# The state product of a linear-attention sequence: one 128-column matmul, or four 32-column tiles of the array

## What is computed

```python
xn = _layernorm(x, axis=-1)
x = x + attn(xn, ...) + ffn(xn, ...)
```

```python
o_int = jnp.einsum('bhtd,bhde->bhte', qc * jnp.exp(gcc)[..., None], S)
kd = kc * jnp.exp(gtc[..., None] - gcc)[..., None]
S = jnp.exp(gtc)[..., None, None] * S + jnp.einsum('bhtd,bhte->bhde', kd, vc)
```

## Time and profile before

| | |
|---|---|
| median of 3 runs | 410.85 us (409.74 to 411.74) |
| profiled execution, its own time | 410.52 us |
| span of its instructions | 408.6 us |
| granted TensorE clock, mean | 0.991 |
| PE busy | 386.7 us (95%) |
| DVE, ACT, POOL busy | 326.3, 304.5, 276.6 us |
| matmuls of the state, L747 | 64 records of 377 ns (median) |
| DVE's copy of the state, L1468 | 32 of 425 ns (median) |

### The profile page before, as it was taken

How to read it: one execution, slowest core, us unless ns; L and a number is a source line. 1 busy time by engine, 2 the same in 40 slices (tenths; PEclk the granted TensorE clock), 3 DMA queues, 4 the chain that set the end, 5 groups by cost and what they waited for, 6 DMA issues and landing times.

```text
span 408.6 us, 13495 instructions
## 1 busy us (share of the span) xinstructions
PE 386.7 (95%) x3650; PEld 337.1 (83%) x3651; DVE 326.3 (80%) x868; ACT 304.5 (75%) x947; POOL 276.6 (68%) x237
## 2 busy tenths in 40 slices
PE   7988899999999999999999999899999999999990
PEld 6656788877788888888888878799999999999990
DVE  5989898999988898889888888667687687687750
ACT  4889998787887978797888887466666676666660
POOL 6012534268888888888888833178888888888884
PEclk9999999999999999999999999999999999999996
DMA  8846586464555445474655340145545555455530
GB/s 237 230 158 193 177 288 245 120 186 129 170 179 162 128 127 168 143 200 140 186 155 154 115 137 14 44 63 69 69 68 65 66 69 67 63 67 71 64 32 0
DMA packets 59096, 51.29 MB, mean 126 GB/s; under 512 B 7200, under 2 KB 51392, under 8 KB 59072
## 3 DMA queue, kind: packets, MB, share of 16 engines
q1 hardware_dynamic: 45936, 42.07, 36.0%
q0 software_dynamic: 12272, 8.54, 15.1%
q10 hardware_dynamic: 864, 0.40, 0.4%
HBM read 33.14 MB, written 18.30 MB: 126 GB/s over the span
## 4 chain that ended last, share of the span: by engine, by line
PE 80%; DVE 6%; ACT 4%; DMA 3%; issue 3%; POOL 2%; SPq 1%; ACTq 0%; DVEq 0%; POOLq 0%
PE psA L912 16%; PE psVG L900 16%; PE psVG L721 9%; PE psO L756 8%; PE psA L737 7%; PE psT L790 6%; PE psQK L709 6%; PE psT L782 4%; PE psKS L747 3%; PE psO L770 3%; ACT E L1080 2%; SPq L343 1%; DMA x_all<-in_L_attn_x_dram 1%; DMA gcB<-decay_rows 1%; PE psQK L891 1%
## 5 line engine op out<-in xcount | busy, mean ns | idle before, releaser
L579 POOL DMA_INDIRECT out_dram<-yw,sidx x71 | 115.0, 1619 | 29.1 <-issue 11.6
L538 POOL TENSOR_TENSOR rms<-msn,neg_half 128x8 f32<-128x8 f32 x32 | 53.3, 1665 | 48.4 <-DVE msn L1412 44.7
L1080 ACT ACTIVATE E<-gcB,ngc 128x128 f32<-128x128 f32 x256 | 78.5, 397 | 0.4 <-DMA gcB<-decay_rows 0.4
L544 POOL DMA_INDIRECT sorted_rows<-x_all,pos_i x64 | 65.2, 1019 | 14.4 <-issue 10.5
L531 POOL TENSOR_SCALAR_AFFINE_SELECT E<-E 128x1024 f32<-128x1024 f32 x32 | 35.7, 1115 | 33.5 <-ACT E L1080 33.2
L756 PEld LDWEIGHTS psO<-v_sb,pr 128*64 128x64 f32 x1024 | 39.8, 137 | 12.0 <-issue 4.1
L756 PE MATMUL psO<-v_sb,pr 128*64 128x64 f32 x1024 | 44.5, 225 | 2.7 <-DVE pr L1440 2.5
L1089 ACT ACTIVATE sq<-psO 128x512 f32<-128x512 f32 x32 | 19.1, 597 | 33.4 <-PE psO L756 33.4
L1440 DVE TENSOR_TENSOR pr<-psA,E 128x512 f32<-128x512 f32 x64 | 41.0, 682 | 0.2
L912 PE MATMUL psA<-xT_all,v_sb 128*128 x288 | 38.3, 276 | 0.5 <-issue 0.4
L900 PE MATMUL psVG<-xgT,gcB 128*128 128x128 f32 x288 | 38.6, 277 | 0.0
(11 more groups left out here) (197 smaller groups left out, 928.5 us busy)
## 6 DMA issues: line engine op xcount, KB each, us to landing
gcB<-decay_rows SPq DMA_DIRECT2D x32, 512.0 KB
sorted_rows<-blank SPq DMA_DIRECT2D x12, 396.0 KB, 5.5
xg<-sorted_rows SPq DMA_DIRECT2D x71, 66.0 KB
x_all<-in_L_attn_x_dram SPq DMA_DIRECT2D x16, 256.0 KB, 5.3
out_dram<-res SPq DMA_DIRECT2D x32, 128.0 KB
eqB<-decay_exp_rows SPq DMA_DIRECT2D x32, 64.0 KB
w1b<-in_L_ffn_w_dram SPq DMA_DIRECT2D x8, 256.0 KB
xT_all<-in_L_ffn_w_dram SPq DMA_DIRECT2D x32, 64.0 KB
```

The source lines that it names most:

```text
L538: nc.gpsimd.tensor_tensor(rms[:], msn[:], neg_half[:, 0:2 * H], ALU.pow).then_inc(rms_ready, 1)
L544: nc.gpsimd.indirect_dma_start(out=sorted_dram, out_offset=bass.IndirectOffsetOnAxis(ap=pos_i[:, t:t + 1], axis=0), in_=x_all[:, t, :], in ...
L579: nc.gpsimd.indirect_dma_start(out=out_rows, out_offset=bass.IndirectOffsetOnAxis(ap=sidx[j][:], axis=0), in_=yw[j][:], in_offset=None, bo ...
L1080: last = nc.scalar.activation(E[j][:, k, h * P:(h + 1) * P], gcB[j][:, k * H + h, :], ACT.Exp, bias=ngcf[:, bass.ds((s * 2 + k) * H + h, 1)])
```

## The change

The one matmul of `state` becomes four, one for each head. Head h has as stationary operand its own 32 columns of `kd` and as moving operand its own 64 columns of `v_sb`; the output goes to partitions 32h to 32h+31 of the bank, so each is a tile of 128 rows and 32 columns of the array. All four write the same 64 columns (256 to 319). Only the last one raises `s_ready`. The three other products of a head's keys with another head's values are not computed any more.

DVE's `copy_state` stays one instruction with the same number of output elements (128x256). It reads the 64 columns four times (a broadcast over the four blocks of `S_sb`) and multiplies with the same mask.

```diff
                 pe.wait_ge(kd_ready, s + 1)
                 pe.wait_ge(v_copied, s + 1)
-                nc.tensor.matmul(psKS[:, HV:2 * HV], kd[:], v_sb[j][:, 0, :], start=True, stop=True).then_inc(s_ready, 1)
+                for h in range(H):
+                    last = nc.tensor.matmul(psKS[h * DK:(h + 1) * DK, HV:HV + DV], kd[:, h * DK:(h + 1) * DK], v_sb[j][:, 0, h * DV:(h + 1) * DV],
+                                            start=True, stop=True)
+                last.then_inc(s_ready, 1)
...
                 dve.wait_ge(s_ready, s + 1)
                 if not (isinstance(i, int) and s == 0):
                     dve.wait_ge(o_ready, s)
-                nc.vector.tensor_tensor(S_sb[:], psKS[:, HV:2 * HV], headmask[:], ALU.mult).then_inc(s_copied, 1)
+                nc.vector.tensor_tensor(S_sb[:].rearrange("p (h d) -> p h d", d=DV), bc(psKS[:, HV:HV + DV].unsqueeze(1), [P, H, DV]),
+                                        headmask[:].rearrange("p (h d) -> p h d", d=DV), ALU.mult).then_inc(s_copied, 1)
```

## The result

The changed kernel took 417.44 us (median of 4 runs, 416.9 to 419.17). The kernel before took 411.3 us beside it (4 runs, 409.74 to 412.12). The ratio is 1.0165, with a 95% interval of 1.0133 to 1.0198: slower by 6 us. The forecast was 410.9, with a range to 413.2, so it was wrong. The same two kernels were later run beside each other three times more. Twice the change cost about the same again (1.0155 and 1.0132), and once it cost nothing (0.998). Why it does both is what the experiments are about; they show where the 6 us go, and leave open what sets it off.

What follows compares the result with a forecast made beforehand. PE was taken as the bound, busy all 90.00 us of the attention window. The profiled 410.52 us, +0.5 for PE and -0.3 for DVE, gave 410.7; with the median 0.33 higher, 410.9, range 408.8 to 413.2.

Steps and rivals of the forecast that it cites:

- The price of the tiles: PE's queue around the state: net +0.01 us per state, between -0.04 and +0.08, taken as +0.5 us in all.
- All three terms: Per state on PE: border into the tiles +0.09 us, state itself -0.18, exposed weight load of the next product +0.10.
- Rival 2: State on PE: no borders or exposed loads, so packing saves 0.32 us each; 401.2 us, chance 0.03.
- Rival 4: State on PE: short tiles run one behind the other, +0.30 us per state; 420 us, chance 0.03.
- What `S_sb` gives: DVE's copy of the state starts 0.18 us earlier, which helps from 77.35 to 93 us: -0.3 us in all.
- In the loop this buys nothing, as PE doesn't wait for DVE there: DVE's copy in the loop: its start, 0.18 us earlier, gains no time.
- ends at 143.61, ahead of its reader on PE: DVE's `res`, in the same chain as the state's copy, is done before the PE line L782 needs it.
- rival 1: Second half of L756: the earlier state clears PE's stalls in some 24 steps, -2.9 us; 408.0 us, chance 0.08.
- Rival 3: Borders around the state cost more, +0.08 us each, 413.3 us; or PE's stalls grow, 413.8; chance 0.15.

Runs made afterwards that it cites:

- `a_again`: The changed kernel, unaltered, run again beside the kernel before at another time: 409.29 us, ratio 0.998.
- `b_again`: The kernel before, unaltered, run again for its trace: 408.82 us, ratio 1.0002.
- `a_third`: The changed kernel, unaltered, run a third time beside the kernel before: 417.39 us, ratio 1.0155.
- `a_fourth`: The changed kernel, unaltered, run a fourth time on one more chip as the yardstick: 417.63 us, ratio 1.0132.
- `e14_shift_before`: The kernel before with the output projection's signal raised by a later matmul, 0.27 us later, same work: 417.09 us, ratio 1.0113.
- `e5_diag`: The changed kernel with its four tiles written in the diagonal blocks and DVE reading 256 columns as in the kernel before: 409.32 us, ratio 1.0012.
- `e3_maskfirst_after`: The changed kernel with POOL's mask moved ahead of the three indirect stores of a step: 431.91 us, ratio 1.0486.
- `e8`: State as one matmul for sequences 0 to 11, four diagonal-block tiles from 12 on, DVE as in the kernel before: 408.74 us, ratio 1.0007.
- `e9`: State as four diagonal-block tiles for sequences 0 to 11, one matmul from 12 on, DVE as in the kernel before: 408.88 us, ratio 1.0003.
- `e12_two_tiles`: The kernel before with projection ahead of the state, two 64-column state tiles, outputs' own halves together, `on` ahead of `S_sb`: 413.14 and 414.57 us.

## Why the prediction was wrong, point by point

**The price of the tiles: right.** All three terms came to within 5 ns (table above): +90, -181 and +105 ns make +14, where +10 was forecast. The step is 6 or 7 ns shorter all the same, since the row from L709 to L721 takes some 24 ns less in `a_again` than in `b_again`; nobody forecast that, and no run says why. That the step comes out so near to no change is in part luck. Rival 2, for which the Trainium skill spoke ("TensorE: Matmul & The Clock Gate", "Measured speedup vs the span model"), is refuted. The rule holds inside the group as far as the stream goes, with the four tiles starting 6 or 7 ns apart here and not 4; it has no term for the changes of shape on either side, 0.09 and 0.09 + 0.10 us, and these eat the gain. Rival 4 is refuted too: eight records take 0.25 with the border.

**What `S_sb` gives: right but small.** It starts 0.15 us earlier against the last L721 (0.705 behind it and not 0.859), where 0.18 was forecast; the 0.3 us can't be seen in the scatter of the start-up stretch.

**The step that failed** is the sentence "In the loop this buys nothing, as PE doesn't wait for DVE there", with the one on `res`, which "ends at 143.61, ahead of its reader on PE". Both are true of the earlier trace rows. But they rest on a signal that arrives as its matmul ends. `res` has some 0.7 us to spare before it delays the transposes, and with the holds of 0.90 to 1.25 us it starts 1.15 to 1.40 us behind the projection and not 0.29, so 0.9 to 1.1 later. I looked at how much work was ahead of each wait and not at how much delay each wait could stand, and who could cause one.

**The second fault** is in rival 1. The profile of before had a hint: stalls of 0.1 to 0.25 us with no work to explain them. I put them down to DVE's and POOL's work lying over L756, and allowed as much change as they had size (2.9 us in either direction). `b_again` shows that they vanish altogether where no signals are held: 6.893 in place of 7.005 us. With the signals of L756 late by 0.07 to 0.47 us in the same profile, I take them for the mild form of the disturbance that became 0.42 us a step (7.308 against 6.887). Rival 3 had its sign and the words "the stalls of rival 1 may also grow", but 2.9 us as an end, and no mechanism.

**Why it tips.** This part is argued and not shown. In the long rhythm the wait may keep the place itself: a step longer by 0.3 to 0.5 us leaves PE so against POOL that the next signal falls into the store too. In the kernel before the signals fell from 0.07 us ahead of the store to 0.18 into it. The change moves the projection's end against the state by -181 + 106 = -75 ns and adds 90 ahead, which is next to nothing against TensorE's own row of work. In undisturbed steps the place is 0.245 us into the store in the changed kernel and 0.22 to 0.24 in the kernel before. So I can't say that these 20 ns cause it. Shown are only the two ends: in three of four comparisons the changed kernel was held from the eleventh step on and stayed so, and the kernel before goes much the same way if its signal is moved by 0.27 us. The first held signal of each run does not fit the place in the store, and nothing here explains it.

**Still open.** What in the chip holds the signals and makes PE pause, and why it was there in the first comparison and beside `a_third`, `a_fourth` and `e14_shift_before`, but not beside `a_again` and `e5_diag`. In the former sets the kernel before took 411.2 to 412.2 us, in the latter 409.2 and 409.6; that this 2 us is the mild form of the hold fits the 0.11 us a step between the two profiles of the kernel before. One rival stands untested: the recording itself. In the profiles of `before`, `after`, `a_third` and `a_fourth` about a third or more of the records of PE's, DVE's and ACT's signals are missing, and all but a few are there where none was held. Against it: `e3_maskfirst_after`, with the longest holds, has 150 of 154. All executions here have a span and a clock of their own, so were recorded; none shows the kernels without it. And the runs without stores take away GpSimd's instruction and all that hangs on it at once. `e5_diag`, `e8` and `e9` were not tried with held signals, so what part the diagonal blocks or DVE's spread read have there wasn't tested.

## What to carry over

Price a tile shape by what stands on both sides of it: a small matmul between two whole-array ones pays two borders of 0.09 us and 0.10 for the next weights, and four packed tiles of 64 columns then only equal one matmul of 256 (within 14 ns here). For each wait of the loop, ask how late its signal may come before the bounding engine stops; here the one for `res` could stand 0.7 us beside GpSimd's indirect stores and got 0.9 to 1.1, which the sum of busy times does not show. Steps of unequal length in a loop of equal work are to be explained, from the semaphore's time against the end of the instruction that raises it, before a change is costed; and a difference of 1.5% can depend on when it is measured, so that both kernels should be run again, beside each other, at another time.

## What the runs showed of the hardware

- PE's completion signals arrived up to 1.48 us after the matmul's end around GpSimd's indirect stores of 128 rows, and up to 3.76 us with three stores one behind the other. PE itself mostly ran on, but paused 0.2 to 0.9 us in some steps. Without the stores no signal was late (0.05 us at most), in the same set of runs. At other times, on the same chip, none was with the stores either.
- Where signals were held, the trace had records of 106 to 116 of some 175 signals of PE in the first profiles, `a_third` and `a_fourth`; without the stores it had all 183.
- Four 32-column tiles of 64 columns, fp32 in two passes, took 0.25 us to the start of the next matmul on the whole array. The tiles start 6 or 7 ns apart, the second pass 80 ns behind the first.
- Two 64-column tiles lost their overlap in some steps of `e12_two_tiles`: 1.05 us for work that takes 0.54 otherwise. I have no cause for it.
